# Layer 0's first loads waited for one by one, layer 1's root products over 32 rows, and last stores that land in the next layer

## The reference

```python
x = x + L0(gn(x))   # retention: qk = (rot(q) rot(k)^T) * mask, divided by clip(sum|qk|, 1, 5e4),
                    #   times v; layer norm over each head's 32 channels, gelu, product with Wo
x = x + L1(gn(x))   # mLSTM: up product, causal convolution of 4 taps, silu, q k v in blocks of 4,
                    #   gates, decayed causal attention in chunks, per-head layer norm
                    #   hn = (h - mu) / sqrt(var + 1e-5) * norm_w, + skip * x_act, * silu(z), down
x = x + L2(gn(x))   # neighbourhood attention, 7x7, with a bias table
x = x + L3(gn(x))   # neighbourhood attention, 7x7, with a soft mask, rms norms, rotary
```

## Time and profile before

| | |
|---|---|
| median of 3 runs | 3328.1 us (3321.17 to 3329.22) |
| profiled execution | 3324.22 us, of which 3322.4 us span from first to last instruction |
| mean granted TensorE clock | 0.955 |
| TensorE busy | 3016.2 us, 91% of the span |
| VectorE busy | 2143.1 us, 65% |
| ScalarE busy | 1994.1 us, 60% |
| GpSimd busy | 1133.1 us, 34% |
| layer 0 | 0 to 1016 us |
| layer 1 | 1016 to 2024 us |
| layer 2 | 2024 to 2563 us |
| layer 3 | 2563 to 3322 us |

### The profile page before, as it was taken

The page is one execution under the profiler, slowest core; times in us unless marked ns, Lnnn a source line. Parts: engine busy times, 40 slices in busy tenths (PEclk is TensorE's granted clock), DMA queues, the critical chain, the costliest instruction groups (busy, mean ns, idle before and its releaser), DMA issues. The chain is left out here.

```text
span 3322.4 us, 103102 instructions
## 1 busy us (share of the span) xinstructions
PE 3016.2 (91%) x43288; PEld 1669.9 (50%) x43288; DVE 2143.1 (65%) x5155; ACT 1994.1 (60%) x4348; POOL 1133.1 (34%) x1441
## 2 busy tenths in 40 slices
PE   6999999999996999999999987989997788888886
PEld 3333333333323656556565555667765455555554
DVE  5887878878864676767667653555454466666664
ACT  2767667676664555564555533555554677777774
POOL 3343433433421322222222211323222455555553
PEclk8999999999997999999999998999998899999997
DMA  6877877778672233233322223555543233333332
GB/s 196 164 175 144 182 170 163 167 171 179 143 180 85 62 85 84 68 87 87 87 69 82 64 68 125 175 169 159 172 144 118 73 90 118 116 117 121 114 104 78
DMA packets 298892, 411.55 MB, mean 124 GB/s; under 512 B 39328, under 2 KB 255808, under 8 KB 277824
## 3 DMA queue, kind: packets, MB, share of 16 engines
q1 hardware_dynamic: 276720, 272.65, 27.3%
q0 software_dynamic: 18000, 131.08, 19.7%
q10 hardware_dynamic: 3712, 1.23, 0.1%
HBM read 219.47 MB, written 53.81 MB: 82 GB/s over the span
## 5 line engine op out<-in xcount | busy, mean ns | idle before, releaser
L859 ACT ACTIVATE l_sizes<-l_probs 128x2048 f32<-128x2048 f32 x256 | 487.0, 1908 | 301.3 <-DVE l_probs L800 293.6
L1936 POOL TENSOR_TENSOR l_logits<-l_logits,l_inv 128x400 f32<-128x400 f32 x256 | 245.0, 958 | 743.4 <-DVE l_inv L1915 737.7
L1929 ACT ACTIVATE l_logits<-l_logits,l_low 128x100 f32<-128x100 f32 x1024 | 372.6, 366 | 208.8 <-DVE l_low L1909 208.3
L301 PE MATMUL l_psum<-shared_x,shared_space 128*128 128x512 f32 x896 | 411.8, 605 | 12.7 <-DVE l_row_var L1482 11.6
L800 DVE TENSOR_TENSOR l_probs<-l_psum,l_decay 128x1024 f32<-128x1024 f32 x256 | 299.7, 1218 | 85.0 <-PE l_psum L674 74.0
L800 DVE TENSOR_TENSOR l_probs<-l_psum,shared_space 128x1024 f32<-128x1024 f32 x256 | 300.3, 1218 | 75.1 <-PE l_psum L674 74.5
L674 PE MATMUL l_psum<-l_qk 32*128 32x512 f32 x2048 | 340.5, 644 | 6.6 <-DVE l_qk L759 3.3
L967 POOL DMA_DIRECT2D l_sizes<-l_sizes x125 | 108.6, 869 | 537.3 <-ACT l_sizes L859 525.3
L1726 POOL TENSOR_TENSOR shared_space<-shared_space,l_causal 128x1024 f32<-128x1024 f32 x64 | 152.8, 2388 | 372.2 <-DVE l_x_act L1424 225.6
L689 PE MATMUL l_psum<-l_probs,shared_x 128*32 128x512 f32 x2048 | 270.6, 600 | 0.2
L301 PEld LDWEIGHTS l_psum<-shared_x,shared_space 128*128 128x128 f32 x896 | 163.8, 192 | 200.3 <-issue 194.4
(11 more groups left out here) (245 smaller groups left out, 5817.8 us busy)
## 6 DMA issues: line engine op xcount, KB each, us to landing
l_sizes<-l_sizes POOLq DMA_DIRECT2D x125, 1024.0 KB, 7.6
l_V_windows<-v_image SPq DMA_DIRECT2D x512, 100.0 KB
l_V_windows<-v_padded SPq DMA_DIRECT2D x512, 100.0 KB
shared_space<-rows_c SPq DMA_DIRECT2D x64, 512.0 KB, 5.9
shared_x<-y SPq DMA_DIRECT2D x24, 1024.0 KB, 5.6
y<-l_res SPq DMA_DIRECT2D x31, 512.0 KB, 3.4
l_e_everywhere<-rows_e SPq DMA_DIRECT2D x112, 128.0 KB, 5.6
shared_x<-x SPq DMA_DIRECT2D x8, 1024.0 KB, 12.2
```

The source lines that it names most:

```text
L301: i = nc.tensor.matmul(out, w[:, k, m * P:(m + 1) * P], act[:, k, n0:n1], start=(k == 0), stop=(k == tiles - 1))
L859: nc.scalar.activation(sizes[:, slot(N), :, :], probs[:, N % 2, :, :], ACT.Abs).then_inc(sized, 1)
L1929: nc.scalar.activation(e, e, ACT.Exp, scale=-1.0, bias=self.low[:, N % 4, i:i + 1], accum_out=self.total[:, N % 4, i:i + 1]).then_inc(self ...
L1936: nc.gpsimd.tensor_tensor(p, p, self.inv[:, N % 4, :].unsqueeze(2).to_broadcast([P, STEP, NKEY]), ALU.mult).then_inc(self.p_ready, 1)
```

## The change

Three things, independent of each other in the code.

- Layer 0: `rest_loaded` is split in three. `values_loaded` counts `wv` and the rotation table, `row_scale_loaded` counts `row_scale`, which is now issued ahead of `wo`, and `rest_loaded` counts the other four (64). VectorE waits for `values_loaded` alone, GpSimd for `values_loaded` and `row_scale_loaded`, ScalarE no longer waits before the values but before the first gelu, and TensorE waits for the rest before the first `var`.
- Layer 1: the root products read rows 32i to 32i+31 of `spread_norm` and `VR` in place of rows 32i and 32i+1. The added rows have zero weights, so the result is the same.
- The last store of layers 0, 1 and 2 counts on a semaphore that outlives the layer, `shared.stored`, and the layer no longer waits for it. In layer 1 the last unit's result is built in `shared.x[1]`, which is free once the last z products have read it; so `load_residual` of that unit waits for the z products. The next layer's SyncE waits for the store before it overwrites or reads what the store reads: in layer 1 after the first loads and `folded`, in layer 2 before the loads of images 1 and 2, in layer 3 between the loads of images 1 and 2.

```diff
-                sp.dma_start(wv[:, :, :], wview(A["L0_WvT"])).then_inc(rest_loaded, 16)
-                sp.dma_start(table[:, :], A["rot_table"]).then_inc(rest_loaded, 16)
+                sp.dma_start(wv[:, :, :], wview(A["L0_WvT"])).then_inc(values_loaded, 16)
+                sp.dma_start(table[:, :], A["rot_table"]).then_inc(values_loaded, 16)
...
-                        sp.dma_start(y[b - 1, :, m, :], of).then_inc(stored, 16)
+                        sp.dma_start(y[b - 1, :, m, :], of).then_inc(stored if k + 1 < HALVES * B else shared.stored, 16)
...
-                sp.wait_ge(stored, 16 * HALVES * B)
+                sp.wait_ge(stored, 16 * (HALVES * B - 1))
...
                         pe.wait_ge(squared, H + 1)
+                        if H == 0:
+                            pe.wait_ge(rest_loaded, 64)
...
-                dve.wait_ge(rest_loaded, 112)
+                dve.wait_ge(values_loaded, 32)
...
+                                       (row_scale[:, :, :].rearrange("p g r -> p (g r)"), A["row_scale"], row_scale_loaded),
                                        (wo[:, :, :], wview(A["L0_WoT"]), rest_loaded),
-                                       (row_scale[:, :, :].rearrange("p g r -> p (g r)"), A["row_scale"], rest_loaded),
...
-                act.wait_ge(rest_loaded, 112)
                 values(0)
...
                         if n == 8 + 2 * g and H > 0:
+                            if H == 1:
+                                act.wait_ge(rest_loaded, 64)
                             gelu(H - 1)
...
-                pool.wait_ge(rest_loaded, 112)
+                pool.wait_ge(values_loaded, 32)
+                pool.wait_ge(row_scale_loaded, 16)
...
+        last_res = shared.x[(B - 1) % 3][:, :, 0:BANK]
...
-                    if f >= 2:
+                    if f + 1 == UNITS:
+                        ring.is_full(sp, ("z", f, 1))
+                    elif f >= 2:
                         sp.wait_ge(stored[f % 2], 16 * (f // 2))
...
                 sp.wait_ge(folded, 1)
+                sp.wait_ge(shared.stored, 16)
...
-                    sp.wait_ge(stored[s], 16 * UNITS // 2)
+                    sp.wait_ge(stored[s], 16 * (UNITS // 2 - s))
...
-                                m = nc.tensor.matmul(out[:, (i % 2) * BANK:(i % 2 + 1) * BANK], spread_norm[32 * i:32 * i + 2, :],
-                                                     VR[n % 2][32 * i:32 * i + 2, :], start=True, stop=True)
+                                m = nc.tensor.matmul(out[:, (i % 2) * BANK:(i % 2 + 1) * BANK], spread_norm[32 * i:32 * i + 32, :],
+                                                     VR[n % 2][32 * i:32 * i + 32, :], start=True, stop=True)
...
+                sp.wait_ge(shared.stored, 32)
                 for b in (1, 2):
                     load(b)
...
-                sp.wait_ge(stored, 32 * B)
+                sp.wait_ge(stored, 32 * B - 16)
...
-                for b in (1, 2):
-                    load(b)
+                load(1)
+                sp.wait_ge(shared.stored, 48)
+                load(2)
```

More of the change, by code:

```diff
@@ L362, in __init__ @@
         self.x = [sb(f"x{s}", [P, HALVES, T]) for s in range(3)]
+        self.stored = nc.semaphore("last_stored").__enter__()
         self.space = sb("space", [P, 8192])
@@ L548, in layer0 @@
         next_loaded = L.sem("next_loaded")
-        first_loaded, rest_loaded, wv_ready = L.sem("first_loaded"), L.sem("rest_loaded"), L.sem("wv_ready")
+        first_loaded, values_loaded, wv_ready = L.sem("first_loaded"), L.sem("values_loaded"), L.sem("wv_ready")
+        row_scale_loaded, rest_loaded = L.sem("row_scale_loaded"), L.sem("rest_loaded")
         def wview(w):
@@ L1123, in by_pair, with residual_of @@
             return ap.rearrange("p (a b) n -> p b a n", b=2)
+        def residual_of(f):
+            return res[f % 2][:, :, :] if f + 1 < UNITS else last_res
         with nc.Block() as block:
@@ L1153, in store @@
                     b, hf = f // 2, f % 2
-                    sp.dma_start(y[b, :, :, hf * BANK:(hf + 1) * BANK], res[f % 2][:, :, :]).then_inc(stored[f % 2], 16)
+                    if f + 1 < UNITS:
+                        sp.dma_start(y[b, :, :, hf * BANK:(hf + 1) * BANK], res[f % 2][:, :, :]).then_inc(stored[f % 2], 16)
+                    else:
+                        sp.dma_start(y[b, :, :, hf * BANK:(hf + 1) * BANK], last_res).then_inc(shared.stored, 16)
                 def load_residual(f):
                     b, hf = f // 2, f % 2
-                    if f >= 2:
+                    if f + 1 == UNITS:
+                        ring.is_full(sp, ("z", f, 1))
+                    elif f >= 2:
                         sp.wait_ge(stored[f % 2], 16 * (f // 2))
-                    sp.dma_start(res[f % 2][:, :, :], x[b, :, :, hf * BANK:(hf + 1) * BANK]).then_inc(res_loaded[f % 2], 16)
+                    sp.dma_start(residual_of(f), x[b, :, :, hf * BANK:(hf + 1) * BANK]).then_inc(res_loaded[f % 2], 16)
                 sp.dma_start(ident[:, :], A["ident"]).then_inc(rest_loaded, 16)
@@ L1517, in residual @@
                     dve.wait_ge(res_loaded[f % 2], 16 * (f // 2 + 1))
-                    nc.vector.tensor_tensor(res[f % 2][:, :, :], res[f % 2][:, :, :],
+                    nc.vector.tensor_tensor(residual_of(f), residual_of(f),
                                             ring.region(name).rearrange("p (m n) -> p m n", m=HALVES), ALU.add).then_inc(ring.took(name), 1)
@@ L2026, in store @@
                     s = slice(half * BANK, (half + 1) * BANK)
-                    sp.dma_start(y[b, :, :, s], norm.x(b)[:, :, s]).then_inc(stored, 16)
+                    last = (b, half) == (B - 1, 1)
+                    sp.dma_start(y[b, :, :, s], norm.x(b)[:, :, s]).then_inc(shared.stored if last else stored, 16)
                 sp.dma_start(wo[:, :, :], A["L2_WprojT"].rearrange("(k p) n -> p k n", k=HALVES)).then_inc(rest_loaded, 16)
```

## The result

| | before | after |
|---|---|---|
| median of the runs | 3324.6 us (3312.8 to 3329.2, 4 runs) | 3278.8 us (3262.1 to 3296.3, 4 runs) |
| profiled execution | 3324.2 us, span 3322.4 | 3278.6 us, span 3276.8 |
| granted clock of TensorE, whole span | 0.955 | 0.965 |

The ratio is 0.9877 with a 95% interval of 0.9842 to 0.9911: the kernel is 1.2% faster, and the time lies 8 us under the forecast of 3287 and inside its range. The two profiled executions differ by 45.6 us, where the sum had 39.5.

A forecast was written before the change was run, and what follows sets the result against it. TensorE, busy 91% of the span, was taken as the bound, losing time standing still or at half clock. Terms 13.2 + 3.0 + 7.3 + 16 = 39.5 us from 3324.2 gave 3284.7, plus 2.0, rounded: 3287; 8-in-10 range 3274 to 3310.

The forecast's parts named there:

- the sum: Whole kernel: start 13.2, clock at the start 3.0, ends of layers 7.3 and root products 16 make 39.5 us.
- The rows: Layer 1's root products: 32 rows in place of two keep TensorE's clock up, 16 us, between 0 and 17.9.
- the rival: Layer 1, main rival in the experiments: the clock's drops do not depend on rows at all; no chance given.
- rival 3: Root products: 32-row products don't run beside each other, 3.60 us a group for 1.14, 39 us more; 2%.
- rival 1: Layer 1: rows don't matter to the clock, or `tok` products alone lower it; gain 23.5 us, 3303; 18%.
- The start: Layer 0: with the waits split, first scores come at 28.9 in place of 42.1 us, a gain of 13.2.
- The clock at the start: Layer 0, first scores to second half batch: full clock once gaps close, 3.0 us, at most 4.7, lower end 0.
- The ends of layers: Borders behind layers 0, 1 and 2: without SyncE's wait for the last store, 7.3 us less in all.
- rival 2: Ends of layers: the barrier waits for the store in flight anyway, 7.3 us don't come, 3294; 8% alone.

The follow-up runs named there:

- e1: The kernel before with only layer 0's first waits split as in the change: 3300.6 us, ratio 0.9936.
- e3: The kernel before with only the last stores handed to the next layer: 3310.7 us, ratio 0.9971.
- e4: The kernel after with the root products back at two rows: 3296.1 us, ratio 0.992.
- e6: The kernel before with 8 rows of each strip in the root products, nothing else changed: 3311.1 us in a single execution.
- e5: The kernel before with 16 rows of each strip in the root products, nothing else changed: 3296.2 us in a single execution.
- e2: The kernel before with only the root products over 32 rows: 3293.9 us, ratio 0.9911.
- e9: The kernel after with two more products, their result unread, in TensorE's gap ahead of the first scores: 3280.9 us, ratio 0.9889.
- e10: The kernel after, unchanged, run once more beside the others: 3272.5 us, ratio 0.9875.
- e11: The kernel after with VectorE's wait for the other first loads put back ahead of the mean of wv: 3285.3 us in a single execution.
- e8: The kernel after with two-row root products and the second half of q's projection moved between root and `tok` products: 3318.3 us, ratio 1.0000.
- e7: The kernel after with the second half of q's projection moved between the root and `tok` products: 3302.2 us, ratio 0.9951.

## Right or wrong, step by step

**The rows: right in mechanism.** All traces but those of the moved projection, by rows in the root products:

| rows | kernels | intervals with a drop | the 13 together, us | mean |
|---|---|---|---|---|
| 2 | before, e1, e3, e4 | 9, 6, 3, 11 of 13 | 758.3, 747.5, 740.6, 761.0 | 751.9 |
| 8 | e6 | 5 | 747.2 | |
| 16 | e5 | 3 | 740.8 | |
| 32 | after, e2, e9, e10, e11 | 3, 1, 4, 1, 1 | 742.0, 733.5, 744.8, 735.8, 735.2 | 738.3 |

With two rows 29 intervals of 52 have a drop, with 32 rows 10 of 65. The intervals of one trace may hang together, so these are nine traces rather than 117 trials. The mean clock of all runs says the same without counting drops, in three pairs that differ in the rows alone: 0.956 and 0.963 (before and e2), 0.960 and 0.965 (e4 and after; 0.966 in e10), 0.956 and 0.965 (e8 and e7). The times of the 13 overlap (740.6 with two rows, 744.8 with 32), which is why one trace of each could not have told, and why e3 looked like the rival. The means differ by 13.6 us, and the whole by 16.1 (e7 and e8), by 27 to 30 (e2) and by 17.3 (e4 to after, in different groups). My term was 16, out of 0 to 17.9. Its parts were off in two ways that cancelled. The first odd interval takes 60.27 us with a drop (after) and 57.63 without (e10), so a drop costs 2.64 us there, where I had 1.56. TensorE's busy time does grow by 1.56 (57.63 - 56.07), but its idle time by another 1.08 (2.64 - 1.56), which I had left out. Within after, where a later interval is the clean one, the difference is 2.97 us, 1.80 of them busy. In the interval with the drop TensorE waits 1.2 us for `row_var` on VectorE, and in the clean one of e10 that wait is missing. The wait, in after:

```profile
PE l_psum L301 <- DVE l_row_var L1499: 1.2, 1, 1.2
```

And the drops did not all go. Three in after, at 2.6 to 3.0 each, gave 8 to 9 us back. So it is luck that the term of 16 came out so near to the 16.3 of the traces. The price of the wide products was 0, as said: 1.14 us for eight with two rows and with 32, which also rules rival 3 out.

Windows of 1 us over all these intervals show where the clock is low: always within the first 9 us behind a group of root products (13 in e8), and nowhere else in an interval. The `tok` products and the small products of the chunk's attention stand there too and stayed as they were; no run changed them, so their share in the drops that are left is open. So is what it is about the 30 added rows, that they are driven at all or that the data on them is not zero.

The rule of the Trainium skill that I had cited (TensorE: Matmul & The Clock Gate, section "Why this matters for your kernels"), not to leave TensorE idle between bursts, would have made this term 0 (rival 1). Taken alone it is not enough: e2_rows changes nothing but the rows, and the mean clock rose from 0.956 to 0.963. The section's statement that a single product over 32 rows takes as long as one over 128 agrees with the trace: the shortest records of the root products (2 rows), of the scores (32) and of the projections (128) in before take 587, 587 and 589 ns.

**The start: 12.75 of 13.2.** Right in its cause (e11) and its place. Two small errors: the keys ended at 20.11 + 3.60 = 23.7 in place of 22.7, and the second half tile of the keys followed at 23.75. From there the scores took 5.6 us and not 6.2. The keys were late because the eight products of the queries took 6.42 us where they had taken 5.32. That is the half speed of the first products again: the first fast load begins at 17.37 in before and at 19.68 in after. It is not the work of VectorE and GpSimd beside them, since in e2_rows and e3_stores, where these stand still then as in before, it begins at 19.51 and 21.10. I had taken the 5.32 us as given. The first decay table (here `shared_space`, issued at about 3 us) and `row_scale` came in time, as said:

```profile
shared_space<-decay SPq DMA_DIRECT2D x1, 3840.0 KB, 15.3
...
l_row_scale<-row_scale ACTq DMA_DIRECT2D x1, 32.0 KB, 6.5
```

**The clock at the start: the step that failed in after.** I had 3.0 us; after shows -0.5: 57.22 us from the first scores to the second half batch, against 56.73 before. The clock did not fall in the gap, where it is 1.00, but just behind it, as the scores had begun (0.80 from 29 to 30 us, then 0.50). The mechanism is there, though. In all seven traces with the early start this stretch has one of two lengths: 53.1 us in four (e1, e7, e9, e10) and 57.2 in three (after, e4, e8). The right term was not 3.0 but either 3.6 or -0.5, and over these seven 1.9. Which of the two came went with the moment at which the first products reached full speed (e10, above). I had named the lower end, the clock that falls in the gap all the same, and should have given the two outcomes near equal weight instead of a value between them.

**The ends of layers: 6.9 of 7.3.** 2.27, 2.35 and 2.30 us, each near the wait that had stood there. The barrier does not wait for a store in flight, so rival 2 is out. The new wait in layer 3 cost 0.3 us of SyncE's time, in layers 1 and 2 none shows.

**What failed, or was not in the sum: layer 2.** No part of the change touches its products. Its time with the border behind layer 2, in before, after and after once more:

```profile
2024.11:2562.86 538.75, 484.42 (x13840) 357.78 (x13841) 270.68 (x1432) 283.17 (x1169) 142.97 (x189) 0.95 0.51 158
```

```profile
1992.84:2518.87 526.03, 477.07 (x13840) 353.48 (x13841) 270.58 (x1432) 283.36 (x1169) 142.95 (x189) 0.96 0.52 162
```

```profile
1975.22:2507.21 531.99, 483.69 (x13841) 356.67 (x13842) 270.49 (x1432) 283.18 (x1169) 142.95 (x189) 0.95 0.51 160
```

VectorE, ScalarE and GpSimd do the same work to 0.3 us; only TensorE's busy time and clock differ. Over all 13 traces this stretch lies between 526.0 and 546.0 us. The edits don't order it: after and e11 have 526.0 and 526.1, after once more 532.0, and e3, which has the last stores moved too, 546.0:

```profile
2004.27:2550.22 545.95, 488.94 (x13841) 358.61 (x13842) 270.92 (x1432) 283.48 (x1169) 142.94 (x189) 0.94 0.50 156
```

So the 10.4 us of after were not an effect of the change that would come again; 4.5 of them were left in the second execution. The same holds for the last pair of layer 1 (57.8 us in after, 55.0 in e10).

**The total.** The forecast of 3287 was 8 us high in the first set. The two sets of runs of after have medians of 3278.8 and 3272.5, the mechanism of each of the three parts was right, and the range held. But part of how well the sum fitted is luck: the ten runs of one kernel spread over 25 to 41 us (e1: 3280.9 to 3321.6), at mean clocks from 0.957 to 0.966. No version tried here beats the kernel after: e9 is not to be told from it, e7 is slower.

## What to carry to other kernels

A wait that counts several loads together releases its engine at the last of them. Read which one the profile names, and split the count where the first user needs only the first loads: it moved the first scores by 12.75 us here, and with VectorE's wait alone put back all of it was lost. A barrier at the end of a layer needs no wait for a store that the next layer neither reads nor overwrites early; this gave 2.3 us a border. Where TensorE is the bound and thin products stand beside a drop of its clock, rows of zero weights in the same strips of 32 cost nothing and keep the clock up more often, but judge it over many runs or many intervals, since one trace of each kernel can show the opposite.

## What the runs showed of the hardware

- The clock of TensorE can fall to 1.2 GHz while the engine has work all the time. How often it does depends on the rows of products nearby, rows of zero weights included: 29 of 52 intervals with two rows, 10 of 65 with 32, at the same 1.14 us for eight products. Moving dense products in between did not help (11 of 13 in e8).
- The clock column of the profile reads 1.00 at the start of a trace although TensorE runs at half speed there: weight loads of 0.34 us every 0.85 us, later 0.19 every 0.43. The step up came between 17.4 and 21.1 us in the traces read for it.
- The same instructions can get either clock: 0.50 and 1.00 in the same 10.2 us of two executions of one kernel, behind the same gap of 2.05 us. In seven traces it held where the step up at the start came by 18.8 us and fell where it came from 19.7 on. In layer 0 this is worth 4.1 us, in layer 2 up to 20 us (526.0 to 546.0).
- An interval bound by TensorE loses more by a drop than the growth of TensorE's busy time: 2.6 us where the busy time grew by 1.56, and 3.0 where it grew by 1.80.
